# Two PSUM evictions of a block attention trade engines: the transposed probabilities go from VectorE to ScalarE, the head outputs from ScalarE to VectorE

## What is computed

```python
qh = jnp.einsum('btd,dhe->bthe', q, wq) + bq
kh = jnp.einsum('btd,dhe->bthe', k, wk) + bk
vh = jnp.einsum('btd,dhe->bthe', v, wv) + bv
scores = jnp.einsum('bqhe,bkhe->bhqk', qh * scale, kh)
scores = jnp.where(causal, scores, NEG_INF)
p = jax.nn.softmax(scores, axis=-1)
o = jnp.einsum('bhqk,bkhe->bqhe', p, vh)
o = jnp.einsum('bqhe,hed->bqd', o, wo) + bo
s = o.reshape(N, L, W_) @ proj_w + proj_b
out = x + s * silu(ffn(layernorm(x)))
```

## Time and profile before

| | us |
|---|---|
| median of 3 runs | 2039.82 |
| lowest and highest of the 3 | 1922.07, 2112.36 |
| the profiled execution, its own time | 1901.07 |
| its span, slowest core | 1899.5 |
| spans of the eight cores | 1887.0 to 1899.5 |

### The profile page before, as it was taken

One profiled execution on the slowest core, in us unless ns is written; L12 is line 12 of the kernel. 1 busy time (PEld: TensorE's weight loads), 2 busy tenths in 40 slices (PEclk: granted clock), 3 DMA queues, 4 the chain that ended last, 5 costly groups with the idle time before them and its releaser, 6 DMA issues.

```text
span 1899.5 us, 17834 instructions; the slowest of 8 cores (1887.0 to 1899.5 us)
## 1 busy us (share of the span) xinstructions
PE 1542.0 (81%) x7424; PEld 726.0 (38%) x7424; DVE 381.2 (20%) x548; ACT 393.7 (21%) x545; POOL 229.3 (12%) x180
## 2 busy tenths in 40 slices
PE   0345799999999999999999999886647656788782
PEld 0244344444444444444444444333424424222220
DVE  2776100000000000000000000002352341247475
ACT  1443000000000000000000000495452443233332
POOL 0000011111111111111111111000000000124244
PEclk9877799999999999999999999997555555687876
DMA  5998666666666666666666666523000006422424
GB/s 138 215 242 167 78 78 73 73 77 77 78 78 75 72 75 78 78 78 74 74 75 77 78 78 73 94 46 88 1 1 0 1 6 118 109 89 89 177 89 177
DMA packets 230822, 163.62 MB, mean 86 GB/s; under 512 B 74691, under 2 KB 222403, under 8 KB 226499
## 3 DMA queue, kind: packets, MB, share of 16 engines
q0 software_dynamic: 155472, 92.97, 38.4%
q1 hardware_dynamic: 75270, 69.50, 13.1%
HBM read 220.69 MB, written 16.78 MB: 125 GB/s over the span
## 4 chain that ended last, share of the span: by engine, by line
PE 62%; DMA 10%; ACT 8%; DVE 8%; POOL 4%; issue 4%; SPq 3%; POOLq 0%; DVEq 0%; ACTq 0%
PE pCv L632 53%; DMA AL<-x 5%; PE pWO L906 4%; DMA AL<-pw 4%; POOL AL L1042 2%; ACT AL L694 2%; POOL AL L1045 2%; SPq L416 2%; PE pQ L716 1%; DVE tStat L320 1%; DVE AL L787 1%; ACT L694 1%; DVE tSc L765 1%; DVE tRs L779 1%; ACT pS L772 1%
## 5 line engine op out<-in xcount | busy, mean ns | idle before, releaser
L632 PE MATMUL pCv<-AL 128*128 128x512 bf16 x4608 | 1002.8, 380 | 1.0 <-DVE tWmT L550 1.0
L632 PEld LDWEIGHTS pCv<-AL 128*128 128x128 bf16 x4608 | 450.0, 98 | 553.7 <-issue 4.4
L765 DVE TENSOR_REDUCE tSc<-pS 128x1 f32<-128x512 f32 x32 | 21.8, 682 | 1196.1 <-PE pS L758 1196.1
L575 POOL DMA_DIRECT2D AL<-cw x144 | 125.9, 875 | 1054.2 <-PE pCv L632 863.0
L647 ACT ACTIVATE AL<-pCv,tCbT 128x512 bf16<-128x512 f32 x48 | 29.0, 687 | 889.2 <-PE pCv L632 889.2
L454 PE MATMUL pLgT<-AL 128*64 128x128 bf16 x768 | 60.4, 258 | 126.9 <-DMA AL<-AL 126.9
L974 PE MATMUL pPr<-AL 128*128 128x512 bf16 x448 | 120.9, 418 | 12.0 <-DVE AL L1022 12.0
L906 PE MATMUL pWO<-AL 64*128 64x256 bf16 x512 | 109.8, 414 | 5.7 <-ACT AL L838 5.7
L454 PEld LDWEIGHTS pLgT<-AL 128*64 128x64 bf16 x768 | 59.4, 137 | 127.8 <-issue 127.8
L799 PE MATMUL pPT<-tI,AL 128*128 128x128 bf16 x128 | 18.7, 300 | 88.5 <-DVE AL L787 88.5
L906 PEld LDWEIGHTS pWO<-AL 64*128 64x128 bf16 x512 | 72.6, 142 | 41.9 <-issue 6.5
(11 more groups left out here) (95 smaller groups left out, 837.1 us busy)
## 6 DMA issues: line engine op xcount, KB each, us to landing
AL<-cw POOLq DMA_DIRECT2D x144, 512.0 KB, 6.0
AL<-x SPq DMA_DIRECT2D x16, 2048.0 KB, 11.8
out<-AL SPq DMA_DIRECT2D x8, 2048.0 KB, 7.2
AL<-pw POOLq DMA_DIRECT2D x8, 1024.0 KB, 8.6
AL<-wq POOLq DMA_DIRECT2D x1, 2048.0 KB, 19.1
AL<-wk POOLq DMA_DIRECT2D x1, 2048.0 KB, 15.9
AL<-wv POOLq DMA_DIRECT2D x1, 2048.0 KB, 15.2
AL<-wo POOLq DMA_DIRECT2D x1, 2048.0 KB, 16.7
```

The costliest lines, as they stand in the source:

```text
L575: sCWs[gi % 4].add(e.dma_start(out=cwr[:, gi % 4, :].rearrange("p (g f) -> p g f", g=8), in_=d_cw[s, g].rearrange("g p f -> p g f")), 16)
L632: ins = e.matmul(p_cv[:, 512 * (bs + 2 * sub + hf): 512 * (bs + 2 * sub + hf) + 512], lhsT, xnTh[:, o:o + 512], start=(step == 0), stop=(s ...
```

## The change

st_pte becomes an activation Copy on ScalarE and st_ote a tensor_scalar add on VectorE; their places in the order are exchanged with them. ScalarE's block of a step is now st_pte(Q-2), st_exp(Q), in this order; VectorE's is st_dve2(Q-1), st_dve1(Q), and in a block behind it st_ote(Q-3). In the tail, ScalarE has one block with st_pte(Qm-1) and another with st_pte(Qm), and VectorE has the three st_ote. No buffer, semaphore or wait value changes.

```diff
-                cPTe.add(e.tensor_copy(pTs[:, sB:sB + 512], p_pT[:, sB:sB + 512]), 1)
+                cPTe.add(e.activation(pTs[:, sB:sB + 512], p_pT[:, sB:sB + 512],
+                                      AF.Copy), 1)
...
-                    cOTe.add(e.activation(
+                    cOTe.add(e.tensor_scalar(
                         dst[0:64, head, 128 * (b % 2):128 * (b % 2) + 128],
                         p_oT[0:64, sB + 128 * i:sB + 128 * i + 128],
-                        AF.Identity, bias=t_bvT[:, head:head + 1]), 1)
+                        t_bvT[:, head:head + 1], None, ALU.add), 1)
...
                         if Q - 1 in Qs:
                             st_dve2(e, Q - 1)
                         st_dve1(e, Q)
+
+                    @AC
+                    def _(e, Q=Q, Qs=Qs):
                         if Q - 2 in Qs:
                             st_pte(e, Q - 2)
-
-                    @AC
+                        st_exp(e, Q)
+
+                    @DV
                     def _(e, Q=Q, Qs=Qs):
-                        st_exp(e, Q)
                         if Q - 3 in Qs:
                             st_ote(e, Q - 3)
...
                 @DV
                 def _(e, Qm=Qm):
                     st_dve2(e, Qm)
+
+                @AC
+                def _(e, Qm=Qm):
                     st_pte(e, Qm - 1)
...
-                @DV
+                @AC
                 def _(e, Qm=Qm):
                     st_pte(e, Qm)
...
-                @AC
+                @DV
                 def _(e, Qm=Qm):
                     st_ote(e, Qm - 2)
                     st_ote(e, Qm - 1)
```

## The result

| | before | changed |
|---|---|---|
| median, us | 1919.57 (10 runs) | 1890.67 (9 runs) |
| lowest and highest | 1899.43, 2112.36 | 1877.92, 2026.42 |
| the profiled execution | 1901.07 | 1884.72 |
| its span, slowest core | 1899.5 | 1883.2 |
| spans of the eight cores, median | 1894.1 | 1872.0 |

In some executions the cores of one die are granted a lower clock and take longer; the others, called undisturbed here, give a ratio of 0.9888 with a 95% interval from 0.9839 to 0.9937: faster by less than 2%, and clear of the noise. By that ratio it is about 21 us; the two medians of the table lie 28.9 apart, since they are taken over all executions. The sum ahead of the result said 23.7 us and a ratio of 1877.4 / 1901.07 = 0.9875.

The account below looks back on a forecast made before the run. It took a ring of waits in the attention steps, no engine full, as the bound; 3 x 6.1 + 5.4 = 23.7 us off gave 1877 us against the profiled execution (1875 to 1885) and 2016 at the median (1870 to 2075).

Parts of the forecast that it names:

- The sum: Over the attention, three groups gain 6.1 us each and the last group 5.4, in all 23.7 us.
- The ring: In the attention steps, a circle of waits between VectorE and ScalarE from row sum to row sum, 5.01 us a turn.
- the same transfers meet: After the attention, the pw loads and a load of x start earlier nearly alike, the latter by 6.1 us.
- The load off the ring: In steps 2 to 7 of a group, the 1.28 us table load moves ahead of the wait for the maximum.
- The adds on VectorE: In the attention loop, four st_ote adds take 1.13 us and make VectorE the bound by 0.12; turn 3.83 us.
- rival B: In the attention steps, slow adds or another wait give a turn of 4.21 us or more, gain 12 to 16; chance 0.13.
- The tail: At the end of three groups, the load before st_pte lies open and the wo projection starts 1.13 us later.
- The last group, other engines: In the fourth group st_quad(31) comes 5.4 us earlier; TensorE and ScalarE have room in a turn of 3.83 us.
- Rival A: In ScalarE's block, Copy and Exp each need a load and the turn stays 5.01 us; 2.8 us slower; chance 0.12.
- Rival C: In the wo projections, denser steps lift TensorE's clock, each losing up to 13.7 us; 65 us gained in all; chance 0.05.
- Rival D: At the pw loads, another overlap makes them a tenth slower and 8 us of the 23.7 are lost; chance 0.05.
- The level and the chances: For the whole time, 2016 us at the median; within 2% 0.82, faster by over 2% 0.13, slower 0.05.

Follow-up runs that it names:

- both counter-experiments: Changed kernel with the exponential ahead of the Copy in ScalarE's block: 1910.61 us; kernel before with a tiny exponential ahead of each exponential's wait: 1881.89 us.

## Why the prediction was right in its mechanism, and where it was wrong

The ring, the load that leaves it and the new bound came as forecast. Two steps failed: the one from the sum to what can be seen of it (the last point), and "the same transfers meet".

- **The load off the ring.** Right, by both counter-experiments. The turn was to be 3.83 us and is 3.80; the Copy behind the load was to end 1.1 us ahead of the maximum's end and does.
- **The adds on VectorE.** Right. Four take 1.10 us, the row of line 787 said 1.13, and the sum starts 1.63 us after the maximum (1.64 said). VectorE is the bound, by the run with six adds; rival B, slow adds, did not come.
- **The tail.** Right in kind: 5.2 us against 5.05 forecast and 3.92 before.
- **The last group, other engines.** Right: the wait of st_ot is gone and TensorE is never late.
- **The sum.** 23.7 forecast, 25.3 measured on every core. About 1.05 of the 1.6 us come from a term that was left out: in each group of the kernel before one row sum comes 0.35 us late, and in the changed kernel none does. The fourth group's starts at 1562.89, when the last st_quad's mask matmul is already running (from 1562.33), and so does not count; three times 0.35 are 1.05. Of the second group, on core 2 of the kernel before:

```profile
1416.46 0.69 DVE L779 TENSOR_REDUCE tRs<-pS 128x4 f32<-128x512 f32 x1 [1.89 <-ACT pS L772]
```

  Its idle time is 1.89 in place of the 1.54 of the earlier trace rows. The rest are turns a few hundredths shorter than forecast and 0.3 at the fourth group's first row sum, which was late before (idle 2.42 in place of 2.14). The late sums are there in the kernels that keep VectorE's copy and give ScalarE an early load or one block. But a turn longer by the same 0.35 also comes once, in the first group, with the exponential first and with six adds, where VectorE has no copy; so the copy alone isn't the cause, and the cause is open.
- **Rival A, two loads in a block.** It did not come: 8 loads at line 772, all in blocks without a Copy. With all of ScalarE's attention in one block a single load is left for Copy, Identity and Exp. The Trainium skill, ScalarE activation tables: per-element evaluation and per-set limits, section Table sets in the compiler and the runtime, says that loads are placed per block; the trace agrees.
- **The drain.** The load at 1328.92 follows the exponential that ends at 1328.90, with no drain between. The prediction set the 1.38 us of the Trainium skill, ScalarE: Activation LUTs, section What ACT_TABLE_LOAD costs, against the loads of the tails. The page gives that drain for a switch to a different set, and these loads bring back the set that is there, so the page's rule did not apply to them and no run here tests it.
- **Rival C, the clock.** The wo projections take 27.46 us as before. The steps are denser and the clock stayed at its lower level of 1.2 GHz.
- **"The same transfers meet."** This step failed. It looked at one core's queue alone: pw behind pw, one load of x. Up to the pw matmuls it held (76.9 to 82.8 us after the first issue, before 77.0 to 80.1). In the last stage the transfers of x meet those of the neighbouring core, and how closely differs by execution, in both kernels. The profile of before has no pair whose first loads of x start within 5 us of each other, the profile of the changed kernel has two (3.5 and 1.8); as far as the runs show, that is chance of the two executions. Of 25.3 us that profiled span kept 16.3, the median over its cores 22, and the quicker pairs of many executions keep 24.9. Rival D named a loss to transfers, but at the pw loads, where there was next to none.
- **The level and the chances.** This step failed, and it made the forecast one of no visible change. It took 2% for the least that can be told from no change, and so put 0.82 on no visible change, though its own sum was 1.2%. The measured interval goes from 0.9839 to 0.9937, half a percent to either side of 0.9888, and leaves out 1: the kernel did get faster. The forecast of the text should have been "faster, by little". It also carried the gain to the median of three runs, 2039.82, and said 2016; over ten runs the median of before is 1919.57, and of the changed kernel 1890.67, 125 us below the 2016. That 1890.67 lies in the stated range of 1870 to 2075 is owed to the range's width and not to the level it was built on. The profiled execution's 1877 was the better centre: the profiled execution of the changed kernel took 1884.72, and the 7 us between them are the 9.0 lost in the last stage less the 1.6 by which the sum fell short.

## What to carry to other kernels

An instruction that no source line asks for can be the longest link of a ring of waits. Here it was 1.28 us of table load at the head of every block of ScalarE's stream, placed behind the wait of the first activation; ask of each load whether it changes the table, and either put the engine's work in one block, or let something that is ready early open the block. Look at what the second of two engines does when the first one's pace changes: the last stage gave back three times the load that was removed. When work is only moved between engines, cost what moves with it; the exchange itself was worth 0.7 us of the stretch where no load was in the way, and cost 11 us where the load stayed on the ring.

## What the runs showed of the hardware

- In these kernels a table load stands ahead of the first activation of each ScalarE block, even if the table is there: 40 loads in the attention of the kernel before (36 of the earlier trace rows and four at the wo evictions), of which 39 fell away in one block. One table serves Copy, Identity and Exp, and one Copy and Silu.
- Such a load of the table that is already there costs 1.28 us and nothing beside it: where nothing waits, activations follow it and precede it within 0.02 us.
- GpSimd's f32 multiplication of 128x1536 takes 3.44 us when it starts first and 6.01 when VectorE starts a 128x2560 one 0.09 us ahead of it; VectorE's takes 2.82 when it is first and 4.95 when GpSimd is 1.2 ahead.
- A 2 MB load issued 0.4 us behind a 2 MB store takes 11.6 to 12.3 us when the neighbouring core starts the same over 5.8 us earlier or later, and up to 16.6 when both start together. From the store's issue to the load's landing the quickest takes 12.0 and the slowest 17.0 us for 4.19 MB, an estimate of 350 and 247 GB/s a core. The Trainium skill, HBM Reference, section Specifications (TRN2), says that the two cores of a pair share one memory's bandwidth, and that a DMA-bound change must be measured with both active. The trace agrees with the pairs; the slower rate of 247 GB/s, where half of the bytes are a store, is below the share that the page gives, about 358 a core.
